# Two scans of eight states per slot instead of four scans of four, in a selective state-space layer

## What is computed

```python
xn = _layernorm(x, axis=-1)
x_and_res = xn @ in_proj_w.T + in_proj_b
x_in = silu(x_and_res[..., :d_model]); res = x_and_res[..., d_model:]
ssm = x_in @ x_proj_w.T + x_proj_b            # dlt_raw (16), Bm (1024), Cm (1024)
delta = clip(softplus(dlt_raw @ dt_proj_w.T + dt_proj_b), 1e-05, 0.1)
A = clip(-exp(A_log), -5.0, -0.01)
# per time step, h is channels x 16:
dA = clip(exp(A * dt[..., None]), 1e-06, 1.0)
h = clip(h * dA + (Bt * dt * xt)[..., None], -100.0, 100.0)
y = sum(h, axis=-1) * Ct + D_param * xt
out = x + (y * silu(res)) @ out_proj_w.T + out_proj_b + ffn(xn)
```

## Time and profile before

| | us |
|---|---|
| median of three runs | 1360.34 (1359.51 to 1361.01) |
| the profiled execution | 1362.2 |
| its span (slowest core; the cores 1356.6 to 1360.7) | 1360.7 |
| VectorE busy | 1329.0 (98%) |
| ScalarE busy | 1191.2 (88%) |
| TensorE busy | 1153.0 (85%) |
| granted TensorE clock, by core | 0.81 to 0.86 |

### The profile page before, as it was taken

How to read it: one execution, slowest core, us unless ns; L and a number is a source line. 1 busy time by engine, 2 the same in 40 slices (tenths; PEclk the granted TensorE clock), 3 DMA queues, 4 the chain that set the end, 5 groups by cost and what they waited for, 6 DMA issues and landing times.

```text
span 1360.7 us, 16801 instructions; the slowest of 8 cores (1356.6 to 1360.7 us)
## 1 busy us (share of the span) xinstructions
PE 1153.0 (85%) x4392; PEld 454.7 (33%) x4392; DVE 1329.0 (98%) x821; ACT 1191.2 (88%) x1900; POOL 72.1 (5%) x101
## 2 busy tenths in 40 slices
PE   5697876899889898889998897798988888887976
PEld 3232332333333333333333332233333333332322
DVE  5899999999999999999999999999999999999997
ACT  3899989989899997999989988999998988789872
POOL 1001100000000000000000000000000000111100
PEclk9777776878777887787877898887877998899979
DMA  9656755555654565455584554554655446454412
GB/s 283 96 108 97 121 107 141 108 104 94 117 113 76 109 120 90 113 111 82 125 124 75 105 115 113 95 108 81 109 110 81 63 78 139 76 142 98 88 48 70
DMA packets 94508, 143.97 MB, mean 106 GB/s; under 512 B 31232, under 2 KB 55360, under 8 KB 94416
## 3 DMA queue, kind: packets, MB, share of 16 engines
q1 hardware_dynamic: 80736, 117.99, 36.1%
q0 software_dynamic: 13680, 24.91, 18.7%
HBM read 101.45 MB, written 35.65 MB: 101 GB/s over the span
## 4 chain that ended last, share of the span: by engine, by line
PE 26%; DVE 26%; issue 22%; ACT 20%; DMA 4%; DVEq 1%; ACTq 0%; SPq 0%
DVE h L747 21%; ACT da L908 12%; PE pS L500 6%; PE pB L467 4%; DMA u<-u 4%; PE pC L477 3%; PE pO L435 2%; PE pX L435 2%; PE pO L511 2%; ACT L908 2%; PE pR L487 1%; PE pO L514 1%; PE pX L511 1%; DVE y L763 1%; PE pX L514 1%
## 5 line engine op out<-in xcount | busy, mean ns | idle before, releaser
L747 DVE TENSOR_TENSOR_SCAN h<-da,u 128x2056 f16<-128x2056 f16 x256 | 1119.3, 4422 | 3.2 <-ACT da L891 1.6
L908 ACT ACTIVATE da<-dl,consb 128x512 f16<-128x512 f16 x1024 | 651.7, 711 | 1.0 <-DVE dl L766 0.2
L500 PE MATMUL pS<-h,eye 128*128 128x512 f16 x1024 | 310.1, 435 | 169.9 <-DVE h L747 169.6
L500 PEld LDWEIGHTS pS<-h,eye 128*128 128x128 f16 x1024 | 100.5, 105 | 347.3 <-issue 313.7
L467 PE MATMUL pB<-xin,wx 128*128 128x512 f16 x512 | 166.1, 484 | 0.6 <-ACT Bf L929 0.6
L477 PE MATMUL pC<-xin,wx 128*128 128x512 f16 x512 | 138.7, 420 | 0.0
L487 PE MATMUL pR<-xnT,win 128*128 128x512 f16 x512 | 135.7, 414 | 0.0
L365 POOL DMA_DIRECT2D yt<-ost x56 | 47.9, 856 | 1048.6 <-ACT ost L969 1016.3
L467 PEld LDWEIGHTS pB<-xin,wx 128*128 128x128 f16 x512 | 54.1, 116 | 94.0 <-issue 82.7
L435 PE MATMUL pO<-xnT,win 128*128 128x512 f16 x304 | 82.0, 419 | 0.0
L908 ACT ACT_TABLE_LOAD x63 | 80.8, 1283 | 1.1
(11 more groups left out here) (144 smaller groups left out, 926.1 us busy)
## 6 DMA issues: line engine op xcount, KB each, us to landing
wo<-wos SPq DMA_DIRECT2D x56, 512.0 KB, 6.5
xt<-x SPq DMA_DIRECT2D x48, 512.0 KB, 6.1
u<-u SPq DMA_DIRECT2D x62, 384.0 KB, 3.2
yt<-xt SPq DMA_DIRECT2D x60, 256.0 KB, 7.8
yt<-ost POOLq DMA_DIRECT2D x56, 256.0 KB, 5.9
wx<-w_x POOLq DMA_DIRECT2D x15, 256.0 KB, 9.2
xnT<-x SPq DMA_DIRECT2D x4, 512.0 KB, 8.9
da<-w_in SPq DMA_DIRECT2D x4, 512.0 KB, 12.3
```

The costliest lines, as they stand in the source:

```text
L500: mm = te.matmul(pS[s % 2][:, :], eye[:, :], h[:, n * SEG + 2:(n + 1) * SEG], start=(n == 0), stop=(n == NST - 1))
L747: v.tensor_tensor_scan(h[:, g * GW:(g + 1) * GW], da[:, g * GW:(g + 1) * GW], u[p][:, :], 0.0, op0=ALU.mult, op1=ALU.add).then_inc(v_scan, 1)
L908: sc.activation(da[:, n * SEG + 2:(n + 1) * SEG], dl[s % 2][:, :], AF.Exp, scale=cc(C_AL + k * NST + n)).then_inc(act_da, 1)
```

## The change

GRP becomes 8. Every slot but 0, 1 and 63 runs two scans of eight states (4112 elements), which `groups` and `scans` count; each is followed by one sum of 8 matmuls. The room comes from other tiles: y1 goes, and y is formed in place in PSUM (pS); t1 lies in the last segment of u; x of the layer norm has one staging buffer instead of two. The copy of u has 7 segments (896 KB) instead of 3 (384 KB). Both carry clips take 8 states, and the clip of the lower half moves ahead of the second scan. `ln_var` moves one slot earlier on VectorE, `ln_nmr` to the next slot. ScalarE runs the upper eight exponentials of s at the head of a step, and the lower eight of s + 1 behind the statistics and ahead of the gate, the silu of x_in, the output and the apply. TensorE runs the sum of the lower half behind R and x_in, and nothing of the slot's own sums between C and R. SP loads x after the transposes.

```diff
-GRP = 4
-NG = NST // GRP
+GRP = 8
...
-            var_at[f + NTT] = c
+            var_at[f + NTT - 1] = c
...
-        t1 = sb("t1", [128, TC], F16)
...
-        y1 = sb("y1", [128, TC], F32)
-        xt = [sb(f"xt{i}", [128, D], F32) for i in range(2)]
+        xt = sb("xtile", [128, D], F32)
...
+        t1 = [u[i][:, (GRP - 1) * SEG + 2:GW] for i in range(2)]
...
+        def groups(s):
+
+            n = 4 if s < 2 or s == NSL - 1 else GRP
+            return [(n0, n0 + n) for n0 in range(0, NST, n)]
+
+        def scans(s, n1=NST):
+
+            return sum(len(groups(q)) for q in range(s)) + sum(n0 < n1 for n0, _ in groups(s))
...
-                if q >= 2:
-                    k2, c2, t2, _ = x_uses[q - 2]
+                if q >= 1:
+                    k2, c2, t2, _ = x_uses[q - 1]
...
-                for q, (_, _, _, su) in enumerate(x_uses):
-                    if su == s + 1:
-                        load_x(q)
                 for (c, m) in out_at[s + 1]:
                     load_wo(c, m)
...
                     transpose(c, t)
+                for q, (_, _, _, su) in enumerate(x_uses):
+                    if su == s + 1:
+                        load_x(q)
...
             def sums(s, g):
-                te.wait_ge(v_scan, s * NG + g + 1)
-                if g == 0 and s >= 2:
-                    te.wait_ge(v_SC, s - 1)
+                n0, n1 = groups(s)[g]
+                te.wait_ge(v_scan, scans(s, n1))
+                if n0 == 0 and s >= 2:
+                    te.wait_ge(v_y, s - 1)
...
                 if 0 <= s < NSL:
                     C_mm(s)
-                    sums(s, 0)
+                    if few:
+                        sums(s, 0)
                     R_mm(s)
...
-                    sums(s, 1)
+                    sums(s, 1 if few else 0)
...
-                if 0 <= s < NSL:
+                if few:
                     sums(s, 2)
...
-                v.tensor_tensor_scan(h[:, g * GW:(g + 1) * GW], da[:, g * GW:(g + 1) * GW], u[p][:, :],
+                    v.wait_ge(pe_s, scans(s - 1, n1))
+                    if keeps(s - 1):
+                        v.wait_ge(v_clo if n1 <= 8 else v_chi, kept(s - 1))
+                v.tensor_tensor_scan(h[:, n0 * SEG:n1 * SEG], da[:, n0 * SEG:n1 * SEG],
+                                     u[p][:, 0:(n1 - n0) * SEG],
                                      0.0, op0=ALU.mult, op1=ALU.add).then_inc(v_scan, 1)
...
-                    v.tensor_mul(y1[:, :], pS[z % 2][:, :], Cf[z % 2][:, :]).then_inc(v_SC, 1)
+                    v.tensor_mul(pS[z % 2][:, :], pS[z % 2][:, :], Cf[z % 2][:, :]).then_inc(v_SC, 1)
...
-                    v.tensor_mul(seg(yb[c % 2], k), y1[:, :], rs[z % 2][:, :]).then_inc(v_y, 1)
+                    v.tensor_mul(seg(yb[c % 2], k), pS[z % 2][:, :], rs[z % 2][:, :]).then_inc(v_y, 1)
...
                     ln_var(var_at[s])
+                if s - 1 in var_at:
+                    ln_nmr(var_at[s - 1])
                 if 0 <= s < NSL:
-                    scan(s, 1)
-                    if s in var_at:
-                        ln_nmr(var_at[s])
-                    if keeps(s):
-                        clip_carry(s, 0, 1)
-                    scan(s, 2)
-                    scan(s, 3)
+                    few = len(groups(s)) == 4
+                    if keeps(s) and not few:
+                        clip_carry(s, 0)
+                    for g in groups(s)[1:-1]:
+                        scan(s, *g)
+                    if keeps(s) and few:
+                        clip_carry(s, 0)
+                    scan(s, *groups(s)[-1])
...
-                if g == (1 if s else 0):
-                    lead(s, 0)
-                if g == 3:
-                    lead(s, 8)
-                for n in range(g * GRP, (g + 1) * GRP):
+                if n0 % 8 == 0:
+                    if s >= 1:
+                        sc.wait_ge(v_scan, scans(s - 1, n0 + 8))
+                    lead(s, n0)
+                for n in range(n0, n1):
...
-                    da_exp(s, NG - 1)
+                    if s == 0:
+                        da_exp(s, 4, 8)
+                    da_exp(s, 8, 16)
...
-                if 0 < s + 1 < NSL:
-                    da_exp(s + 1, 0)
-                if s in var_at:
-                    ln_rstd(var_at[s])
...
+                if 0 < s + 1 < NSL:
+                    da_exp(s + 1, 0, 8)
+                if s in var_at:
+                    ln_rstd(var_at[s])
...
-                if 0 <= s + 1 < NSL:
-                    da_exp(s + 1, 1)
+                for (c, m) in xin_at[s]:
+                    silu_x(c, m)
+                for (c, i) in wf_at[s]:
+                    wf_evac(i)
...
-                if len(ap_at[s]) < 2 and 0 <= s + 1 < NSL:
-                    da_exp(s + 1, 2)
+                    apply(c, t, xt[:, :], xn[:, :])
```

## The result

The changed kernel takes 1391.7 us in the median, the kernel before beside it 1360.47: a ratio of 1.0227, with a 95% interval of 1.0214 to 1.0240. It is 31 us slower; the forecast was 5 us faster, and the range ended at 1365.

What follows compares the result with a forecast made beforehand. VectorE's instruction stream was taken to bound the kernel. Terms -7.3 - 5.3 + 1.0 + 4.2 + 1.0 + 1.5 = -4.9 us gave 1357.3 us profiled, 1355.4 as median; range 1348 to 1365.

Steps and rivals of the forecast that it cites:

- What bounds the kernel: Whole kernel: from the first scan on, time is VectorE's instruction stream; edits count through it or waits opened in it.
- Scans: VectorE, slots 2 to 62: 122 fewer scan instructions save 0.06 us each, -7.3 us (bounds nothing to 9.8).
- D: Rival, VectorE: a scan of eight costs two of four, so only waits go; 1363 us, chance 0.05.
- The sums' slack: VectorE's waits for the summed states and before a scan are covered by the longer scans: -5.3 us.
- In-place y: VectorE's short operations reading and writing PSUM: +1 us, bounds 4.2 us either way.
- ScalarE's new order: ScalarE's reordered steps make VectorE wait: +4.2 us at ln_var, +1 us at the first slot's lower half.
- L: Lateness with which ScalarE begins a slot after the apply slots; 0 to 1.5 us at ln_var, taken as 0.7.
- ln_var: VectorE, fourth statistics slot: ln_var waits for late ScalarE statistics, 0.7 us six times (chunks 2 to 7), +4.2 us.
- The copies of u: Copy of u, seven segments: lands in 4.7 us (7.5 if proportional), within a scan of 8.6; costs nothing.
- First chunk: First chunk: weights issued later behind u, TensorE waits in some four slots, ln_var of slot 3 late: +1.5 us (0 to 5).
- C: Rival, chunk's last slot: TensorE's lower clock level and late output; 1380 us at worst, 1368 at half; chance 0.13.
- B: Rival: ScalarE's lateness, at ln_var and the first slot's lower half, takes the gain; 1361 us, chance 0.17.

Runs made afterwards that it cites:

- e10: e7_best with one edit undone: first chunk's weights again asked for once u has landed; 1357.23 us, 0.9961 of the kernel before.
- e7_best: e1_moved plus ln_var behind second scan, tensor-train weight matmuls behind sums, last chunk's early products spread, first chunk's weights asked earlier; 1362.97 us.
- e1_moved: Changed kernel, other work plan: first x_in pair in a chunk's first slot, sixth slot's output in the seventh; 1367.22 us, 1.0039 of kernel before.
- e11: e10 with scans of four states in slots 2 to 6 too; 1360.57 us, 0.9990 of the kernel before.

## Why the prediction was wrong, step by step

- *What bounds the kernel.* Right: VectorE's stream and the waits in it. All of the loss that could be placed is waits, and with them gone (e10) the kernel is 0.4% faster.
- *Scans.* Right in kind; 0.06 us an instruction was 0.049, 7.3 us was 6.0. A slot without clips takes 19.96 us (582.48 to 602.44) where 19.94 was forecast, so D falls.
- *The sums' slack.* Wrong. I set 8.6 us against the time of 8 matmuls, and took it that TensorE would come to them in time. It comes to them behind an output, and that output waits: 13.1 us in 7 places instead of none. The term of -5.3 us was too large by itself, too: 1.35 us of it is the wait at the last product, which no version loses.
- *In-place y.* Right: +1 us was forecast, the trace gives at most 0.6 (2.71 to 2.73 us from the product to what follows the short operations against 2.72) and the run alone nothing that can be measured. The rule of the Trainium skill that I weighed (page "VectorE: DVE Perf Modes", section "The TRN2 errata — SBUF-src ops pay a fixed extra latency per instruction") doesn't show here: the gate multiply takes 683 ns from SBUF and 684 from PSUM.
- *ScalarE's new order: the step that failed.* I walked ScalarE through the apply slots and found L from the last slot alone, "ScalarE in its order waits for the last one". I counted TensorE's matmuls up to the output and left out what they wait for. `out_mm` calls `wait_bank`. By my own step costs for a slot without statistics (0.1 + 1.5 + 4.9 + 2.4 + 5.0 + 1.3 + 0.6) the silu that frees its bank begins at 15.8 us and ends at 16.4, while 57 matmuls at 0.262 us bring TensorE to the output at 14.9. Neither sum had the other engine's term, and so a ring of two in-order engines stayed hidden. It costs 3.1 to 5.4 us a chunk in six chunks, 28.9 in all with the 1.1 between them. The wait at the first slot's lower half, for which I allowed 1 us, didn't come.
- *ln_var.* 4.0 us of waits against my 4.2, but that is luck: 2.3 of them fell in the first chunk, and the steady chunks, for which the 4.2 stood, had 1.7. Removed from the changed kernel they are worth nothing.
- *The copies of u.* 4.7 us were forecast, the median was 5.3, the longest 7.0, and no scan of the changed kernel waits for one. The 8.2 us that I named as the deciding point were crossed in e7_best, where weights moved beside it, and at one place in e1_moved, e10 and e11.
- *First chunk.* +1.5 (0 to 5) was 7.1: the msq wait there was foreseen, the 4.8 us at a sum was the bank again, by `wf_mm`.
- *The rivals.* C had the right place in part (late outputs, ScalarE waiting, the exponentials behind it) but put it in a chunk's last slot and on the clock. The mean granted clock of after was higher than before; the lower level shows behind the bank's wait, as part of the ring. C's sum was wrong too: 36 less 11 is 25 us slower, so 1385 at the worst and not 1380. B's waits at ln_var, 1.5 to 2 us each in its sum, were 0.4 to 0.5 us in the steady chunks. The chance of 0.19 for slower was too low in my judgement, above all because no rival asked which waits of TensorE ScalarE's new order moves.

## What to carry to other kernels

When an engine's order is changed, list for each instruction that moves back what its completion frees, a PSUM bank above all, and who waits for that; a count of the work on each engine does not show it. An engine that waits for a bank and another that waits for the output in it, both in order, turned 3.1 us of lateness into waits of up to 6 us here. A plan that never puts two users of a bank beside a third in one slot cost nothing that could be measured in this kernel and took nearly all of that back; only with it, and with the smaller edits of e10, was the kernel with the larger scans 0.4% faster than the kernel before.

## What the runs showed of the hardware

A scan costs 8.625 us for 4112 elements a partition and 4.337 us for 2056: all but 0.049 us of it grows with the elements. A multiply or multiply-add of 512 fp32 elements takes VectorE the same time, within 10 ns, whether it reads and writes PSUM or SBUF. I had not expected how little TensorE's mean clock had to do with the result: the kernel before took 1361.36 us in a run with 0.89 granted on every core and 1363.16 in one with 0.81 to 0.84, and the changed kernel, among the slowest, shows 0.88 to 0.89. The stretch matters, though: 0.50 behind each of the long waits for the bank, where eight matmuls take 3.57 us instead of 1.89. A copy of 896 KB inside SBUF landed in 4.5 to 7.0 us in the changed kernel and three in 11.2 to 12.4 where weights moved beside them (e7_best).
